# Four score banks at the end of attention, router logits in quarters, and a second sort at the end of the shared stage

## Chip, core and metric

One core of one Trainium2 chip runs the whole program in one launch. The metric is the device time of that core in microseconds.

## What is computed

The input is one sequence of 2048 tokens with 256 features. Two layers run on it; each has an attention part and a feed-forward part, and each part is behind a layer norm that is modulated by a row made from a condition vector, with a gate on its output. In short:

```python
# layer 0; sa, ca, ga, sb, cb, gb come from silu(c0) @ wmod0
h = layernorm(x) * (1 + ca) + sa
x = x + ga * (softmax_attention(h, Wq, Wk, Wv, biases, 16 heads of 16) + h)
h = layernorm(x) * (1 + cb) + sb
probs = softmax(h @ router_w.T)                      # 8 experts, the best 2 of each token, weights renormalised
moe = sum over the 2 experts e of w_e * (silu(h @ gate_e) * (h @ up_e)) @ down_e       # 176 hidden
shared = (silu(h @ s_gate + bg) * (h @ s_up + bu)) @ s_down + bd                       # 352 hidden
x = x + gb * (moe + shared)
# layer 1: relu attention from the first 32 tokens, then a product with a binarised 256 x 256 weight
```

## The kernel before

The tokens are 16 tiles of 128, in 4 chunks of 512 (NC = 4, TPC = 4 tiles a chunk). Attention runs in NU = 16 units: chunk of queries c = u // 4 and group of four heads g = u % 4. A unit has MT = 16 steps t, one for each tile of keys; in this text such a step of the attention is "tile t of unit u". In one, TensorE computes four score products (L683, one for each head, 512 columns, one PSUM bank each), ScalarE takes their exponentials into prob (L1197), and TensorE multiplies the last tile's prob with the values (weigh, L717, or weigh_half, L724, in two halves of 256 columns put between the scores). Beside them TensorE computes score products once more for the maxima (L653) of a unit ahead, and VectorE reduces them (L1419), five tiles ahead (LEAD = 5). The maxima use banks 0 to 3, the scores banks 4, 5 and 6 in turn, and the output gathers in bank 7. In unit 14 the maxima end after tile 10, as there is no unit 16. Unit 15 has none, and its scores go over four banks (4, 5, 6, 3); its first score waits for all exponentials of unit 14. Units 2 to 12 have the product with the values in halves; units 0, 1, 13, 14 and 15 don't.

Each engine works through its queue in the order in which the program is written; semaphores tie the engines together. At the end of attention the next stages begin beside it. The order is written out by hand in hooks (beside_last_but_one, beside_last, beside_shared), and for a chunk c of 512 tokens it is:

- VectorE: statistics(1, c), then POOL: deviation(1, c) (L1970, L1972), then VectorE: normalise(1, c), which writes xh1 (L1359). There is one xh1, so each chunk's comes after the last one's readers.
- TensorE: turn1(c, ft), transposes of xh1 (L778), twice a chunk. VectorE: halves(c, ft) reads them and writes hT_hi and h32 (L1497, L1500). POOL: input_rest(c), the low half hT_lo (L2137).
- TensorE: logits(c), 24 small products of 8 columns each (L800). VectorE: router_logits(c), ScalarE: router_exp(c), VectorE: router_ranks(c) and shares(c).
- POOL: tokens_by_row(c), the rows that are later scattered to the experts' slots.

Beside that, POOL gates and adds the attention of each unit (gate_attention, add_attention, L2060); between the two, SP moves it with 16 small DMAs (move_attention, L402). In the middle of unit 14 POOL also rounds the experts' down weights (down_rounded, L2118 and L2120).

The shared stage has ST * NC = 12 steps n (three parts of the hidden units of each chunk). In each, TensorE computes hidden(sg) and hidden(su) (L837) and the down product of the step before (L858), ScalarE the gate (L1222) and the rounding of the hidden tile (L1227), VectorE the product (L1668) and the low half (L1672). Beside it stand: sort(0) (TensorE at step 1: L871 and L874; VectorE at the same step), chunk 3's statistics, normalise, turns (steps 4 and 5), logits (step 7) and ranks (step 8), and sort(1) (TensorE at step 9, VectorE at step 10). sort(part) counts the chosen tokens of each expert and gives every token its slots: sort(0) for chunks 0 to 2, sort(1) for chunk 3. POOL scatters the rows with indirect DMAs (place, L2180): 24 for part 0, 8 for part 1; after the first six it makes chunk 3's deviation, after 14 chunk 3's input_rest.

Then follow 46 expert tiles (31 of part 0 and 15 of part 1) in a pipeline over all engines: load (xg), transposes (turn_in, L907), gate and up (gate_up, L935), the product (gated_tile, L1686), transposes (turn_hidden, L949), down (down_tile, L961). Beside tiles 8, 10 and 12 TensorE computes the modulation rows of layer 1 (row1, bank 5 or 1) from wmod1. After that come the gather of the results and layer 1.

Bank 4 holds both sorts in turn, then the turned hidden tiles; bank 2 the logits of chunks 0 to 2 and, from step 0 of the shared stage, the up products; bank 5 the turns and logits of chunk 3.

## Time and profile before

| what | us |
|---|---|
| median of 3 runs | 1047.78 (1047.33 to 1050.42) |
| the profiled execution's own time | 1047.59 |
| span in its profile | 1045.8 |
| mean granted TensorE clock | 0.944 of 2.4 GHz |
| units 0 to 15 of attention, first score to the last transpose of output | 105.3 to 772.0 |
| shared stage, up to the first expert tile | to 851.3 |
| expert tiles, up to the last turn of a hidden tile | to 980.3 |

The span is from the first to the last instruction; the execution's own time holds 1.8 us more. In a timeline a row gives start, duration, engine, line, operation, output<-inputs, count, and in brackets the time that the engine sat idle before it and what ended the idling. PE is TensorE, DVE VectorE, ACT ScalarE, POOL GpSimd, SP the engine that only issues DMAs.

### The profile page before, as it was taken

Reading aid. Unit: us, or ns where it says so; the run is one execution under the profiler, and the core shown is the slowest. Engines: PE = TensorE matmul, PEld = TensorE weight load, DVE = VectorE, ACT = ScalarE, POOL = GpSimd, SP = SyncE. Lnnn points to the kernel's source line nnn. Section 1 sums busy time; section 2 is a strip of 40 time slices with the busy share of each in tenths; the row PEclk is TensorE's granted clock in tenths of the full one; section 3 lists DMA queues with packets and bytes.
Section 4 is the critical chain, followed back from the end, with each engine's and each line's share of the span. In section 5 each row is a group of like instructions: output and inputs, shape, how many; then the busy total and the mean of one; then the engine's idle time right before and its main releaser. Section 6 shows DMA issues by size and latency. Waiting matters only on the chain. (4 is left out here: it accounts for less than half of the span.)

```text
span 1045.8 us, 19112 instructions
## 1 busy us (share of the span) xinstructions
PE 988.8 (95%) x6968; PEld 499.5 (48%) x6968; DVE 857.4 (82%) x1162; ACT 675.3 (65%) x1316; POOL 307.4 (29%) x347
## 2 busy tenths in 40 slices
PE   6998999999999999999999999999997889997867
PEld 5453433333333333333333333333456768996656
DVE  5488799999999999999999999987456464655786
ACT  2423777888888888888888888774753224553312
POOL 3285864000000221000000000047437620045553
PEclk8999899999999999999999999996898879997888
DMA  6799200033110110110111101300002224444211
GB/s 197 216 152 134 99 16 6 20 92 106 39 40 6 40 40 7 38 32 16 37 27 21 37 9 39 67 6 1 6 5 70 74 84 144 128 123 135 88 49 60
DMA packets 90129, 65.54 MB, mean 63 GB/s; under 512 B 48406, under 2 KB 77942, under 8 KB 89462
## 3 DMA queue, kind: packets, MB, share of 16 engines
...
q10 hardware_dynamic: 1632, 1.58, 0.5%
...
## 5 line engine op out<-in xcount | busy, mean ns | idle before, releaser
L1197 ACT ACTIVATE prob<-ps 128x512 f32<-128x512 f32 x1024 | 544.6, 599 | 127.7 <-PE ps L683 114.8
L1419 DVE TENSOR_REDUCE mxp<-ps 128x2 f32<-128x1024 f32 x480 | 576.9, 1220 | 22.2 <-PE ps L653 17.4
L683 PE MATMUL ps<-qst,kst 50*128 50x512 f32 x1024 | 374.6, 458 | 5.2 <-DMA qst<-nmT 3.5
L653 PE MATMUL ps<-kst,qst 48*128 48x512 f32 x960 | 328.3, 452 | 0.0
L683 PEld LDWEIGHTS ps<-qst,kst 50*128 50x128 f32 x1024 | 159.7, 190 | 255.2 <-ACT prob L1197 224.6
L724 PE MATMUL ps<-prob,vp 128*32 128x256 f32 x2464 | 196.8, 391 | 0.0
L653 PEld LDWEIGHTS ps<-kst,qst 48*128 48x128 f32 x960 | 130.6, 186 | 14.6 <-issue 6.5
L717 PE MATMUL ps<-prob,vp 128*32 128x512 f32 x816 | 115.6, 640 | 0.0
L724 PEld LDWEIGHTS ps<-prob,vp 128*32 128x32 f32 x2464 | 48.5, 108 | 113.6 <-issue 60.9
L2049 POOL TENSOR_TENSOR att_u<-o_x,rec 128x256 f32<-128x256 f32 x16 | 9.9, 620 | 224.4 <-DVE rec L1444 224.2
L1992 POOL CAST nmp<-nmx 128x16 fp32r<-128x16 f32 x16 | 3.1, 196 | 243.9 <-DVE nmx L1423 218.2
L1686 DVE TENSOR_TENSOR hdt<-ps,sgt 128x176 f32<-128x176 f32 x46 | 15.7, 341 | 49.2 <-ACT sgt L1252 36.4
L1472 DVE TENSOR_REDUCE mxp<-ps 128x2 f32<-128x1024 f32 x32 | 39.2, 1227 | 15.1 <-PE ps L751 15.1
L2210 POOL DMA_INDIRECT yg<-y_slots,slots x32 | 32.1, 1004 | 40.6 <-DVE x L1754 18.5
L1252 ACT ACTIVATE sgt<-ps 128x176 f32<-128x176 f32 x46 | 14.6, 317 | 45.3 <-PE ps L935 36.3
L1359 DVE TENSOR_SCALAR xh<-x,mv,rs 128x256 f32<-128x256 f32 x56 | 34.0, 670 | 9.6 <-POOL rs L1972 9.4
L935 PE MATMUL ps<-gu_hi,th 128*128 x92 | 36.3, 394 | 2.5 <-issue 1.9
L961 PE MATMUL ps<-d_hi,hh 88*128 x92 | 31.3, 340 | 3.7 <-ACT ysb L1265 3.7
L935 PE MATMUL ps<-gu_hi,tl 128*128 x92 | 31.4, 341 | 0.0
L935 PE MATMUL ps<-gu_lo,th 128*128 x92 | 31.3, 340 | 0.0
L1265 ACT ACTIVATE ysb<-ps 128x256 f32<-128x256 f32 x46 | 17.7, 384 | 20.7 <-PE ps L961 16.0
L717 PEld LDWEIGHTS ps<-prob,vp 128*32 128x32 f32 x816 | 16.4, 110 | 28.5 <-ACT prob L1197 18.5
...
## 6 DMA issues: line engine op xcount, KB each, us to landing
...
att_t<-att_u SPq DMA_DIRECT2D x256, 8.0 KB, 1.8
```

The source lines that it names most:

```text
L653: last = nc.tensor.matmul(ps[:, 2 * p + b, :], qst[rows, g, a, P * j:P * (j + 1)], kst[rows, GP * g + a, CH * m:CH * (m + 1)], start=True, ...
L683: nc.tensor.matmul(ps[:, bank, :], kst[rows, GP * g + k // 2, P * t:P * (t + 1)], qst[rows, g, k // 2, :], start=True, stop=True).then_inc ...
L717: last = nc.tensor.matmul(ps[VW * k:VW * (k + 1), 7, :], vp[:, g, t, k, :], prob[:, t % 2, k, :], start=t == 0, stop=t == MT - 1)
L724: last = nc.tensor.matmul(ps[VW * k:VW * (k + 1), 7, cols], vp[:, g, t, k, :], prob[:, t % 2, k, cols], start=False, stop=False, skip_grou ...
L935: last = nc.tensor.matmul(ps[:, 2 + i % 2, 0:2 * I], a[:, i % 2, k, :], b[:].rearrange("p e k n i -> p (e k n i)")[:, bass.ds(e * GW + k * ...
L961: last = nc.tensor.matmul(ps[:, 6, 0:D], a[:, i % 2, n, :], b[:].rearrange("p e n d -> p (e n d)")[:, bass.ds(e * (2 * D) + n * D, D)], st ...
L1197: nc.scalar.activation(prob[:, t % 2, k, :], ps[:, banks[((u * MT if len(banks) == 3 else 0) * G + G * t + k) % len(banks)], :], ACT.Exp, ...
L1265: nc.scalar.activation(ysb[:, i % YB, :], ps[:, 6, 0:D], ACT.Copy).then_inc(yv_s, 1)
L1359: nc.vector.tensor_scalar(dst, x_cols(t), mean, rs, ALU.subtract, ALU.mult).then_inc(xh_s, 1)
L1419: nc.vector.tensor_reduce(own, ps[:, 2 * p:2 * p + 2, :], AX.X, ALU.max).then_inc(mx_read, 1)
L1472: nc.vector.tensor_reduce(own, ps[:, 2 * p:2 * p + 2, :], AX.X, ALU.max).then_inc(mx_read, 1)
L2210: nc.gpsimd.indirect_dma_start(yg[:, m % YG, :], None, y_slots[part], bass.IndirectOffsetOnAxis(ap=slots[:, TPC * d + j, k:k + 1], axis=0) ...
```

## The change

- Attention, units 13 and 14: the products with the values come in halves, for tiles 2 to 15 of unit 13 and 2 to 10 of unit 14.
- Banks: from tile 11 of unit 14 (score 940, RING4) the scores go over four banks (5, 6, 4, 3) without a break into unit 15. The first use of bank 3 waits for the last maximum. The wait for all exponentials at the start of unit 15 is gone.
- Logits of chunks 0 and 1: one tile of 128 tokens (six products) after each of four tiles of unit 15, in place of 24 products after one. The turns of chunk 1 stand one tile earlier. ScalarE's exponentials for the router stand at tiles 7 and 15, in place of 4 and 12.
- VectorE normalises chunk 1 ahead of the logits of chunk 0, and chunk 2 ahead of the logits of chunk 1.
- Logits of chunk 2 go to bank 5, not 2, so that the first up product of the shared stage no longer waits for them to be read; the first turn of chunk 3 into bank 5 does.
- Logits of chunk 3: half before and half after the down product of step 7.
- POOL: chunk 3's deviation after two scatters in place of six.
- Second sort: on TensorE at step 11 in place of 9, in bank 5 at column 128, without the wait for the first sort's slots; on VectorE after the last step, ahead of the first gated tile. The waits for its slots move to the first row1 product.
- SP loads wmod1 without waiting for the second scatters.

```diff
@@ -67,6 +67,7 @@
 QD = 32
 NQ = P // QD
 MAX_LOADS = 2 * NQ
+RING4 = (NU - 2) * G * MT + G * (MI - LEAD)
 
 
 def build(nc, x_in, wq, bq, wk, bk, wv, bv, routerT, gate_w, up_w, down_w, sg_w, sg_b, su_w, su_b,
@@ -325,6 +326,12 @@
         def x_cols(t, n=1):
 
             return x[:].rearrange("p t d -> p (t d)")[:, bass.ds(t * D, n * D)]
+
+        def score_bank(n):
+            return (4, 5, 6)[n % 3] if n < RING4 else (5, 6, 4, 3)[(n - RING4) % 4]
+
+        def sort_cols(part):
+            return (4, 5)[part], 128 * part
 
         END = TPC * (NC - 1)
 
@@ -528,7 +535,6 @@
                     load_tile(i + 6)
                 if i in (0, 2, 4):
                     cols = slice(CH * (i // 2), CH * (i // 2 + 1))
-                    sp.wait_ge(placed[1], 16 * 2 * PARTS[1][1])
                     sp.dma_start(wmod1_sb[:, :, cols], wmod1_v[:, :, cols]).then_inc(mod1_in, 16)
                 if i == 16:
                     sp.wait_ge(row_ps, 3)
@@ -654,7 +660,7 @@
                                             kst[rows, GP * g + a, CH * m:CH * (m + 1)], start=True, stop=True)
                 last.then_inc(mx_ps, 1)
 
-            def unit(u, g, ahead, first=False, beside=None, banks=(4, 5, 6), halved=()):
+            def unit(u, g, ahead, first=False, beside=None, halved=()):
 
                 pe.wait_ge(nm_in, (u + 1) * (16 * MAX_LOADS))
                 for t in range(MT):
@@ -670,17 +676,15 @@
                     pairs = v * (2 * MI) + 2 * i
 
                     def score(k):
-                        n = G * t + k
-                        done = u * (G * MT) + n
-                        bank = banks[(done if len(banks) == 3 else n) % len(banks)]
-                        if len(banks) == 3 and done >= 3:
+                        done = u * (G * MT) + G * t + k
+                        if done == RING4 + 3:
+                            pe.wait_ge(mx_read, NU * (2 * MI))
+                        elif done > RING4 + 3:
+                            pe.wait_ge(p_s, done - 3)
+                        elif done >= 3:
                             pe.wait_ge(p_s, done - 2)
-                        elif n >= len(banks):
-                            pe.wait_ge(p_s, done - len(banks) + 1)
-                        elif n == 0 and not first:
-                            pe.wait_ge(p_s, done)
                         rows = slice(HALF * (k % 2), HALF * (k % 2) + KR + NM)
-                        nc.tensor.matmul(ps[:, bank, :], kst[rows, GP * g + k // 2, P * t:P * (t + 1)],
+                        nc.tensor.matmul(ps[:, score_bank(done), :], kst[rows, GP * g + k // 2, P * t:P * (t + 1)],
                                          qst[rows, g, k // 2, :], start=True, stop=True).then_inc(sc_ps, 1)
 
                     def next_maxima(p):
@@ -769,7 +773,7 @@
             pe.wait_ge(q32_s, len(ITEMS) - EASY)
             unit(0, 0, 2, first=True)
 
-            for u in range(1, NU - 3):
+            for u in range(1, NU - 2):
                 unit(u, u % NG, 2, halved=range(2, MT) if u >= 2 else ())
 
             def turn(q, ft, bank, src):
@@ -786,13 +790,14 @@
             def hT_pair(part, k, c):
                 return (hT_hi[:, c, k, :], hT_lo[:, (c * KT + k) * CH:(c * KT + k + 1) * CH])[part]
 
-            def logits(c, bank, col):
-
-                pe.wait_ge(h_lo_s, KT * (c + 1))
-                pe.wait_ge(tables_s, 2)
-                if c:
-                    pe.wait_ge(lg_s, c)
-                for j in range(TPC):
+            def logits(c, bank, col, tiles=range(TPC)):
+
+                if 0 in tiles:
+                    pe.wait_ge(h_lo_s, KT * (c + 1))
+                    pe.wait_ge(tables_s, 2)
+                    if c:
+                        pe.wait_ge(lg_s, c)
+                for j in tiles:
                     n = 0
                     for k in range(KT):
                         tokens = slice(P * j, P * (j + 1))
@@ -800,9 +805,8 @@
                             last = nc.tensor.matmul(ps[:, bank, col + E * j:col + E * (j + 1)], a[:, tokens], b[:, k, :],
                                                     start=n == 0, stop=n == 3 * KT - 1)
                             n += 1
-                last.then_inc(lg_ps, 1)
-
-            unit(NU - 3, 1, 2)
+                if TPC - 1 in tiles:
+                    last.then_inc(lg_ps, 1)
 
             def beside_last_but_one(t):
                 if t == 15:
@@ -811,18 +815,18 @@
             def beside_last(t):
                 if t == 0:
                     turn1(0, 1)
-                if t == 2:
-                    logits(0, 2, 0)
-                if t in (7, 8):
-                    turn1(1, t - 7)
-                if t == 10:
-                    logits(1, 2, 32)
+                if 2 <= t < 6:
+                    logits(0, 2, 0, (t - 2,))
+                if t in (6, 7):
+                    turn1(1, t - 6)
+                if 10 <= t < 14:
+                    logits(1, 2, 32, (t - 10,))
                 if t in (13, 14):
                     turn1(2, t - 13)
 
-            unit(NU - 2, 2, 1, beside=beside_last_but_one)
-
-            unit(NU - 1, 3, 0, beside=beside_last, banks=(4, 5, 6, 3))
+            unit(NU - 2, 2, 1, beside=beside_last_but_one, halved=range(2, MI - LEAD))
+
+            unit(NU - 1, 3, 0, beside=beside_last)
 
 
             PASSES = ((0, 0), (0, 1), (1, 0))
@@ -865,14 +869,13 @@
 
                 t0, tiles = PARTS[part]
                 pe.wait_ge(chosen_s, (t0 + tiles) // TPC)
-                if part:
-                    pe.wait_ge(slot_s, part)
+                bank, col = sort_cols(part)
                 flat = chosen[:].rearrange("p t e -> p (t e)")
-                nc.tensor.matmul(ps[:, 4, 0:E * tiles], before_bf[:], flat[:, E * t0:E * (t0 + tiles)], start=True, stop=False,
-                                 skip_group_check=True)
+                nc.tensor.matmul(ps[:, bank, col:col + E * tiles], before_bf[:], flat[:, E * t0:E * (t0 + tiles)], start=True,
+                                 stop=False, skip_group_check=True)
                 for t in range(tiles):
-                    last = nc.tensor.matmul(ps[:, 4, E * (t + 1):E * (tiles + 1)].rearrange("p (t e) -> p t e", e=E), ones_bf[:],
-                                            chosen[:, t0 + t, :].unsqueeze(1).to_broadcast([P, tiles - t, E]),
+                    last = nc.tensor.matmul(ps[:, bank, col + E * (t + 1):col + E * (tiles + 1)].rearrange("p (t e) -> p t e", e=E),
+                                            ones_bf[:], chosen[:, t0 + t, :].unsqueeze(1).to_broadcast([P, tiles - t, E]),
                                             start=False, stop=t == tiles - 1, skip_group_check=True)
                 last.then_inc(sort_ps, 1)
 
@@ -883,19 +886,21 @@
             pe.wait_ge(p_s, NU * G * MT)
             weigh(NG - 1, MT - 1)
             hidden((sg_hi, sg_lo), 0, 1).then_inc(g_ps, 1)
-            logits(2, 2, 64)
+            logits(2, 5, 64)
 
             def beside_shared(n):
                 if n == 1:
                     sort(0)
                 if n in (4, 5):
-                    if n == 5:
+                    if n == 4:
+                        pe.wait_ge(lg_s, NC - 1)
+                    else:
                         pe.wait_ge(h_full_s, KT * (NC - 1) + 1)
                     turn(ln(1, NC - 1), n - 4, 5, xh1)
                 if n == 7:
                     pe.wait_ge(h_full_s, KT * NC)
-                    logits(NC - 1, 5, 0)
-                if n == 9:
+                    logits(NC - 1, 5, 0, range(0, TPC // 2))
+                if n == 11:
                     sort(1)
 
             def turn_in(i):
@@ -911,12 +916,12 @@
                 if n >= 2:
                     pe.wait_ge(t_s, n - 1)
                     hidden((sg_hi, sg_lo), 0, n).then_inc(g_ps, 1)
-                if n == 0:
-                    pe.wait_ge(lg_s, NC - 1)
                 hidden((su_hi, su_lo), 2, n).then_inc(u_ps, 1)
                 beside_shared(n)
                 if n >= 1:
                     down(n - 1)
+                if n == 7:
+                    logits(NC - 1, 5, 0, range(TPC // 2, TPC))
 
             pe.wait_ge(t_s, ST * NC - 1)
             turn_in(0)
@@ -944,7 +949,7 @@
                 if i:
                     pe.wait_ge(hl_s, i)
                 else:
-                    pe.wait_ge(slot_s, 2)
+                    pe.wait_ge(slot_s, 1)
                 for n in range(2):
                     last = nc.tensor.transpose(ps[0:IH, 4, P * n:P * (n + 1)], hdt[:, i % 2, IH * n:IH * (n + 1)], ident[:])
                 last.then_inc(ht_ps, 1)
@@ -966,6 +971,7 @@
 
             def row1(j):
                 if j == 0:
+                    pe.wait_ge(slot_s, 2)
                     pe.wait_ge(t_s, ST * NC)
                     pe.wait_ge(mod1_in, 48)
                     pe.wait_ge(cb_ready, 2)
@@ -1186,7 +1192,7 @@
                 act.wait_ge(lg_s, c + 1)
                 nc.scalar.activation(pr[:], lg[:], ACT.Exp).then_inc(exp_s, 1)
 
-            def unit(u, first, ahead, exps={}, banks=(4, 5, 6)):
+            def unit(u, first, exps={}):
                 for t in range(MT):
                     if t in exps:
                         router_exp(exps[t])
@@ -1194,14 +1200,12 @@
                         act.wait_ge(sc_ps, u * (G * MT) + G * t + k + 1)
                         if k == 0 and not (first and t < 2):
                             act.wait_ge(pv_s, u * MT + t - 1)
-                        nc.scalar.activation(prob[:, t % 2, k, :], ps[:, banks[((u * MT if len(banks) == 3 else 0) * G + G * t + k) % len(banks)], :], ACT.Exp,
+                        nc.scalar.activation(prob[:, t % 2, k, :], ps[:, score_bank(u * (G * MT) + G * t + k), :], ACT.Exp,
                                              scale=DH ** -0.5).then_inc(p_s, 1)
 
-            unit(0, True, 2)
-            for u in range(1, NU - 2):
-                unit(u, False, 2)
-            unit(NU - 2, False, 1)
-            unit(NU - 1, False, 0, exps={4: 0, 12: 1}, banks=(4, 5, 6, 3))
+            for u in range(NU - 1):
+                unit(u, u == 0)
+            unit(NU - 1, False, exps={7: 0, 15: 1})
 
             def gate_up_rounded(i):
 
@@ -1553,8 +1557,9 @@
                 t0, tiles = PARTS[part]
                 s, first_tile = sorts[part], TILES[0] * part
                 own_rank = rank[:, t0:t0 + tiles, :]
-                earlier_tokens = ps[:, 4, 0:E * tiles].rearrange("p (t e) -> p t e", e=E)
-                tokens_of = ps[:, 4, E * tiles:E * (tiles + 1)]
+                bank, col = sort_cols(part)
+                earlier_tokens = ps[:, bank, col:col + E * tiles].rearrange("p (t e) -> p t e", e=E)
+                tokens_of = ps[:, bank, col + E * tiles:col + E * (tiles + 1)]
                 first = s["first"]
                 dve.wait_ge(sort_ps, part + 1)
                 rt_then(nc.vector.scalar_tensor_tensor(s["over"][:], tokens_of.unsqueeze(2).to_broadcast([P, E, tiles]), 1.0 / P,
@@ -1600,18 +1605,20 @@
             statistics(1, 1)
             dve.wait_ge(zero_in, 16 * ZERO_DMAS)
             dve.wait_ge(tables_s, 3)
-            router(0, 2, 0)
+            normalise(1, 1)
+            router_logits(0, 2, 0)
+            both_halves(1)
+            router_ranks(0)
             shares(0)
-            normalise(1, 1)
-            both_halves(1)
             statistics(1, 2)
-            router(1, 2, 32)
+            normalise(1, 2)
+            router_logits(1, 2, 32)
+            both_halves(2)
+            router_ranks(1)
             shares(1)
-            normalise(1, 2)
-            both_halves(2)
             leave_output(NU - 1)
             invert_sums(NU - 1)
-            router(2, 2, 64)
+            router(2, 5, 64)
 
             def gate_up_rest(i):
 
@@ -1654,9 +1661,6 @@
                     router_ranks(NC - 1)
                 if n == 9:
                     gate_up_rest(3)
-                if n == 10:
-                    sort(1)
-
             for n in range(ST * NC):
                 s = n % ST
                 rows = S_ROWS[s]
@@ -1870,6 +1874,7 @@
             shares(NC - 1)
             add_shared(NC - 1)
             input_rest(1)
+            sort(1)
             for i in range(TS + 2):
                 if i < TS:
                     gated_tile(i)
@@ -2181,9 +2186,9 @@
                             x_slots[part], bass.IndirectOffsetOnAxis(ap=slots[:, PARTS[part][0] + t, k:k + 1], axis=0),
                             h_tm[part][:, t, :], None).then_inc(placed[part], 16)
 
-            place(0, range(0, 3))
+            place(0, range(0, 1))
             deviation(1, NC - 1)
-            place(0, range(3, 7))
+            place(0, range(1, 7))
             pool.wait_ge(sc_ps, G * MT * NU)
             input_rest(NC - 1)
             place(0, range(7, PARTS[0][1]))
```

## Rows read from the trace of the kernel before

**Rows 1.** The page, part 1: busy us, share of the span, instructions

```profile
PE 988.8 (95%) x6968; PEld 499.5 (48%) x6968; DVE 857.4 (82%) x1162; ACT 675.3 (65%) x1316; POOL 307.4 (29%) x347
```

**Rows 2.** Windows: length, busy us (instructions) by engine, PEclk, DMA share, GB/s

```profile
704.40:724.80 20.40, 19.03 (x67) 5.41 (x67) 16.11 (x7) 9.57 (x19) 15.67 (x6) 0.50 0.01 1
...
796.60:803.30 6.70, 3.77 (x17) 3.76 (x18) 4.53 (x8) 1.30 (x2) 5.41 (x6) 0.50 0.23 80
...
834.10:840.80 6.70, 6.70 (x27) 5.83 (x28) 3.95 (x4) 1.32 (x2) 0.00 (x0) 0.50 0.00 0
```

**Rows 3.** VectorE's timeline, units 11 to 13 end: start us, us

```profile
593.16 0.71 DVE L1440 STREAM_TRANSPOSE o_x<-ps 128x512 f32<-128x512 f32 x1
...
633.11 0.71 DVE L1440 STREAM_TRANSPOSE o_x<-ps 128x512 f32<-128x512 f32 x1
...
674.84 0.71 DVE L1440 STREAM_TRANSPOSE o_x<-ps 128x512 f32<-128x512 f32 x1
```

**Rows 4.** ScalarE's timeline, 703 to 757 us; idle before in brackets

```profile
703.61 2.06 ACT L1197 ACTIVATE prob<-ps 128x512 f32<-128x512 f32 x4 [0.55 <-PE ps L683]
...
707.61 2.08 ACT L1197 ACTIVATE prob<-ps 128x512 f32<-128x512 f32 x4 [1.94 <-PE ps L683]
...
735.36 8.11 ACT L1197 ACTIVATE prob<-ps 128x512 f32<-128x512 f32 x16 [0.75 <-PE ps L683]
...
755.56 2.06 ACT L1197 ACTIVATE prob<-ps 128x512 f32<-128x512 f32 x4 [5.16 <-PE ps L683]
```

**Rows 5.** Timelines of POOL, VectorE and TensorE around chunk 0, 705 to 721 us

```profile
710.25 8.87 POOL L2120 TENSOR_TENSOR d_lo<-d_raw,d_hi 88x4096 fp32r<-88x4096 f32 x1
...
705.73 13.86 DVE L1359 TENSOR_SCALAR xh<-x,mv,rs 128x256 f32<-128x256 f32 x4 [1.58 <-POOL rs L1972]
...
719.64 1.12 PE L778 MATMUL ps<-ident,xh 128*128 128x128 f32 x4 [0.59 <-DVE xh L1359]
```

**Rows 6.** Timelines of POOL and TensorE, second logits and chunk 2

```profile
747.38 0.74 POOL L2060 TENSOR_TENSOR x<-x,att_t 128x256 f32<-128x256 f32 x1 [12.06 <-DMA att_t<-att_u]
...
750.75 0.27 PE L800 MATMUL ps<-rw_hi,hT_hi 128*128 128x8 f32 x1 [0.76 <-POOL hT_lo L2137]
...
763.91 0.63 PE L778 MATMUL ps<-ident,xh 128*128 128x128 f32 x4 [1.73 <-DVE xh L1359]
```

**Rows 7.** Timelines of TensorE, VectorE and POOL in the shared stage

```profile
776.10 0.79 PE L837 MATMUL ps<-hT_hi,su_hi 128*128 128x512 f32 x1 [0.74 <-DVE lg L1516]
...
791.70 0.38 DVE L1344 BATCH_NORM_AGGREGATE mv<-bn_st 128x2 f32<-128x6 f32 x4
...
796.91 1.05 POOL L1972 TENSOR_TENSOR rs<-veps,m 128x4 f32<-128x4 f32 x1
...
799.53 1.12 PE L778 MATMUL ps<-ident,xh 128*128 128x128 f32 x4 [5.35 <-DVE xh L1359]
...
811.86 1.30 POOL L2137 TENSOR_TENSOR hT_lo<-h32b,hT_hi 128x512 fp32r<-128x512 f32 x1
...
814.83 0.17 PE L800 MATMUL ps<-rw_hi,hT_hi 128*128 128x8 f32 x1
```

**Rows 8.** Timelines of ScalarE and TensorE, steps 8 and 9

```profile
827.66 0.69 ACT L1222 ACTIVATE sig<-ps,bg 96x512 f32<-96x512 f32 x1 [7.37 <-remote]
...
834.07 0.21 PE L871 MATMUL ps<-chosen,before_bf 128*128 128x32 bf16 x1 [4.84 <-DVE chosen L1534]
```

**Rows 9.** Timelines of VectorE and TensorE, second sort and first tiles

```profile
844.58 0.18 DVE L1560 SCALAR_TENSOR_TENSOR over<-ps,count 128x32 f32<-128x32 f32 x1
...
847.33 0.16 DVE L1577 TENSOR_SCALAR owner<-ends 1x15 int32<-1x15 f32 x1
...
848.92 0.74 PE L858 MATMUL ps<-sd_hi,hid_hi 96*128 96x256 f32 x4 [1.36 <-ACT hid_hi L1227]
...
853.81 0.34 DVE L1686 TENSOR_TENSOR hdt<-ps,sgt 128x176 f32<-128x176 f32 x1 [0.73 <-issue]
...
856.06 0.63 PE L949 MATMUL ps<-ident,hdt 128*88 128x128 f32 x2
```


## The prediction

> **What bounds the kernel now.** I read the page first. TensorE is busy 95% of the span, VectorE 82%, ScalarE 65% [rows 1]. That is an average over stages, and the change touches only the stretch from about 633 to 860 us, so the other views were read for that stretch alone.
>
> The stage windows show the granted clock. From 704.4 to 724.8 us, the tail of unit 14 and the head of unit 15 of the attention, it is 0.50, which is 1.2 GHz. So it is in windows of 6.7 us in the shared stage [rows 2]. In each of them TensorE waits or has just waited.
>
> The starts of the transposes of attention output give the length of a unit. Unit 12, with the product in halves, takes 633.11 - 593.16 = 39.95 us. Unit 13, without halves, takes 674.84 - 633.11 = 41.73 us [rows 3]. So 14 halved tiles save 1.78 us, 0.127 us a tile.
>
> ScalarE's timeline shows the three banks. In unit 14's tail, at the low clock, a tile takes 1.94 us of idle and 2.08 of exponentials, 4.0 us. In unit 15, on four banks already, 16 exponentials run without a gap in 8.11 us, 2.03 us a tile. Around the second logits ScalarE is idle for 5.16 us [rows 4].
>
> The rows that decide most are those on what TensorE waits for when a normalised chunk is turned. xh of chunk 0 takes VectorE 13.86 us for four small operations, and it ends, at 719.59, just after POOL's rest of the down weights, which alone takes 8.87 us. TensorE turns the chunk at 719.64 after only 0.59 us of waiting [rows 5]. The other waits stand below with their steps.
>
> **The change, part by part.** The profiled execution took 1047.59 us by its own time, 1.8 over its span of 1045.8. The median of the runs shown is 0.2 above it. The sum is made against 1047.6, and 0.2 is added at the end.
>
> *Halves in units 13 and 14.* 14 tiles of unit 13 and 9 of unit 14 at 0.127 us [rows 3] make 1.78 + 1.14 = 2.9 us. VectorE's last maximum comes that much earlier, and with it the deviation, xh and POOL's rounding, which all hang on it. Bounds: 2.5 to 3.2. I take 2.9.
>
> *Four banks from tile 11 of unit 14.* ScalarE's tile 12 ends at 703.61 + 2.06 = 705.67 [rows 4]. Halves and two tiles of 2.03 in place of 2.61 bring that to 701.6; three more tiles and the product behind them, and TensorE would reach the turn of chunk 0 near 708.5. But the turn needs xh, and xh ends with POOL's rounding, at 719.6 - 2.9 = 716.7 [rows 5]. TensorE stands idle for some 8.2 us, and the four banks give nothing there. What is late next is everything behind the turn: the rest of chunk 0, the first logits, the tokens by row, the gate of unit 14. Value 0; bounds 0 and 8.2 gained.
> The Trainium skill, page "SBUF — State Buffer", section "Who interferes with whom", says that a VectorE operation in a two-port mode and a POOL operation lock a shared port pair for a whole instruction, and that the later one is blocked. By that rule the order on the two engines would have to change to free xh, and it doesn't; the trace agrees, since xh ends where POOL does. Were there no lock, the sum would be 8.2 us lower.
>
> *The last unit, up to the second logits.* These wait for POOL's rest of chunk 1, which stands behind the addition of unit 14's attention at 747.38, for which POOL idles 12.06 us while SP moves it in 16 DMAs [rows 6]. That chain is counted from the turn of chunk 0 and holds no work of TensorE's that the change shortens. So the first quarter starts at 750.75 - 2.9, as now. The first logits in quarters and the earlier xh of chunk 1 fill time that is then waited for: TensorE is there some 3 us early. Value 0, bounds -1 and +1.
>
> *From the second logits to the turn of chunk 2.* Now 763.91 - 750.75 = 13.16 us, the last 1.73 of it idle for xh [rows 6], since VectorE normalises chunk 2 only after ranks and shares. With the change xh comes first, and between lie four quarters and three tiles. ScalarE's idle 5.16 us [rows 4] less TensorE's own 0.76 makes 1.1 us a quarter, partly at 1.2 GHz; I estimate 0.7 at the full clock. Three tiles at 2.03 and four quarters make 8.9 us; with a window of 6.7 us at half rate in it, 12.2. I take 10.2, which is 3.0 gained, bounds 1 and 4.3.
>
> *Logits of chunk 2 in bank 5.* The wait of 0.74 us ahead of the first up product goes [rows 7]. Sort and first down product behind it need the ranks and the rounded hidden tile, which hang on the same logits; 0.3 at most gets through. Counted as 0.
>
> *Deviation of chunk 3 after one tile's scatters instead of three.* TensorE waits 5.35 us for xh at 799.53. VectorE's statistics end at 792.08 and POOL's deviation only at 797.96, behind six scatters [rows 7]. With four scatters fewer, xh comes some 3.6 us earlier, allowing VectorE its work between. But the last logits, at 814.83, need POOL's rest of chunk 3, which ends at 813.16 [rows 7] behind 14 scatters in all, in either order. POOL even idles 0.9 us for the statistics. So TensorE meets the wait again ahead of the logits, some 4 us of it. Kept: the 1.67 us of slack less 0.9, 0.7 us; bounds 0 and 3.
>
> *Second sort on TensorE at step 11, not 9.* TensorE waits 4.84 us for the ranks, because ScalarE's gate of step 8 came after 7.37 us of a wait that the trace puts down as remote [rows 8]. Without the sort there, the down product of step 8 needs the rounded hidden tile, some 0.7 us after TensorE gets there if ScalarE is as late again: 4.1 gained. The low-clock window behind the wait, 6.7 us [rows 2], costs 3.4; I count half, 1.7, since another can arise behind the new wait ahead of the logits. Together 5.8, bounds 1 and 8.2.
>
> *Second sort on VectorE at the stage's end.* The idle 1.36 us ahead of the last down product goes, as its hidden tile waited for the sort: 1.4 gained. In its new place the sort, 844.58 to 847.49, so 2.9 us, stands ahead of the first gated tile. That one is ready at 854.15 and is wanted at 856.06 [rows 9], so its turn is 1.0 us late, and the tiles behind it as much. 1.0 lost, bounds 0 and 2.9. POOL's second scatters move with the sort by some 9 us; the first tile that reads them is number 31 of 46. SP no longer waits for them ahead of wmod1, which is wanted at tile 8: hidden either way, and at worst nothing, since the wait only goes. The wait for the second slots now stands ahead of the first row product, at tile 8, past the sort by six tiles: hidden.
>
> Sum: 2.9 + 0 + 0 + 3.0 + 0 + 0.7 + 5.8 + 1.4 - 1.0 = 12.8 us. 1047.6 - 12.8 + 0.2 = 1035.0 us. The tile stage and the end behind it move as a whole.
>
> **The rivals.**
> *The tail opens* (0.10). xh isn't the bound, or TensorE no longer idles and the clock stays up. For it: tiles of 2.03 us in unit 15 [rows 4]. Against it: rows 5. It gives up to 8.2 us more: 1026.8 us. The page "TensorE: Matmul & The Clock Gate" of the Trainium skill, section "Terms", puts the penalty at the throttled time times the share taken away; for the windows of rows 2, 33.8 us, that is an estimate of 17 us, if all went. The trace doesn't bear this out, as in the tail half of each tile was a wait between engines.
>
> *The waits only move in the shared stage* (0.20). POOL's 12 scatters in a row, and last logits split by a down product, make the last ranks as late as before, and the stall of step 9 turns up at step 8 or 11. The 5.8 goes: 1040.8 us.
>
> *Only the halves count* (0.08). Each later gain ends at a wait for POOL, and 2.9 us or little more is left: 1045 us.
>
> *The clock stays low* (0.04), the slower side. TensorE's idle 8.2 us ahead of the turn leaves it at 1.2 GHz, and unit 15 never brings it back. A tile at that clock takes 4.0 us with its waits, 2.0 over ScalarE's 2.03; four banks take away about half of that. 1.0 us over 16 tiles, and 24 router matmuls twice at twice their price, lose some 20 us: 1055 us. It turns the sign from 13 tiles at the low clock. Against it: the clock was back 5.2 us after the turn at 719.64, and 3.8 us after the wait of 5.35 [rows 2, 5, 7].
>
> **How the numbers follow.** The forecast has 0.58. The range leaves out half of the opened tail (0.05) below, and above it "only the halves", the low clock and a little of the moved waits (0.15): 1028 to 1042. Within 0.3% (3.1 us, about what a measurement here can tell from no change) means above 1044.6, half of "only the halves" and a little of the moved waits. That makes faster 0.90, same 0.06, slower 0.04.
>
> **What would show it.** In the changed profile: transposes of attention output 1.8 us closer for unit 13; ScalarE's tiles at 2.03 in unit 14's tail; then TensorE idle 7 to 9 us for xh, its turn near 716.7; the second logits near 748; the turn of chunk 3 after 1 to 2 us of waiting, and a new wait for POOL's rest ahead of the last logits; no wait at the second sort; a gap ahead of the first turn of a hidden tile. I am wrong if xh isn't waited for, if the last logits don't wait, or if more than two low-clock windows come or go.

## The result and the profile after

The changed kernel takes 1052.57 us (median of 18 runs, 1049.37 to 1057.86), the kernel before 1047.49 in its 18 runs of the same comparison. The ratio is 1.0057, with a 95% interval of 1.0041 to 1.0073: slower by 0.57%, some 6 us, where 12.8 us less was forecast. The profiled execution took 1053.04 us, with a span of 1051.3.

The page, part 1, of the changed kernel. TensorE is busy for 979.4 us, 9.4 less than before [rows 1], in a longer span: it makes the same products (more of them in halves) and waits more.

```profile
PE 979.4 (93%) x7152; PEld 495.2 (47%) x7152; DVE 869.1 (83%) x1162; ACT 678.6 (65%) x1316; POOL 307.8 (29%) x347
```

What was forecast for the halves is there. Timelines of TensorE, VectorE and POOL around chunk 0, which answer to [rows 5]:

```profile
714.60 1.11 PE L782 MATMUL ps<-ident,xh 128*128 128x128 f32 x4 [8.89 <-DVE xh L1363]
...
700.74 13.80 DVE L1363 TENSOR_SCALAR xh<-x,mv,rs 128x256 f32<-128x256 f32 x4 [1.58 <-POOL rs L1977]
...
705.26 8.81 POOL L2125 TENSOR_TENSOR d_lo<-d_raw,d_hi 88x4096 fp32r<-88x4096 f32 x1
```

Counted from the transpose of unit 12's output, TensorE turns chunk 0 after 83.78 us, before after 86.53. It waits 8.89 us for xh (8.2 forecast). The clock is at 1.2 GHz then, but back at 2.4 GHz some 6 us after the turn.

At the second logits, those of chunk 1, it goes wrong for the first time. TensorE's timeline, and ScalarE's, which answers to [rows 4]:

```profile
746.08 0.37 PE L805 MATMUL ps<-rw_hi,hT_hi 128*128 128x8 f32 x1 [3.23 <-POOL hT_lo L2142]
...
751.83 1.22 PE L687 MATMUL ps<-qst,kst 50*128 50x512 f32 x4
752.98 1.93 PE L721 MATMUL ps<-prob,vp 128*32 128x512 f32 x8
754.85 0.38 PE L805 MATMUL ps<-rw_hi,hT_hi 128*128 128x8 f32 x1
...
756.22 1.22 PE L687 MATMUL ps<-qst,kst 50*128 50x512 f32 x4
...
760.54 1.11 PE L782 MATMUL ps<-ident,xh 128*128 128x128 f32 x4
```

```profile
748.28 2.07 ACT L1203 ACTIVATE prob<-ps 128x512 f32<-128x512 f32 x4 [4.86 <-PE ps L687]
752.66 2.06 ACT L1203 ACTIVATE prob<-ps 128x512 f32<-128x512 f32 x4 [2.32 <-PE ps L687]
757.05 2.06 ACT L1203 ACTIVATE prob<-ps 128x512 f32<-128x512 f32 x4 [2.32 <-PE ps L687]
```

The windows of the changed kernel (length, busy us and instructions by engine, PEclk, DMA share, GB/s). They answer to [rows 2].

```profile
744.40:764.90 20.50, 18.82 (x78) 9.18 (x79) 3.81 (x13) 8.37 (x17) 8.79 (x7) 0.50 0.00 1
706.80:720.50 13.70, 5.90 (x24) 2.63 (x24) 10.68 (x6) 2.06 (x4) 8.54 (x2) 0.50 0.00 0
```

In the first of them the clock is at 1.2 GHz for 20.5 us, though TensorE never idles again from 746.08 to its end. A tile there takes 756.22 - 751.83 = 4.39 us, its products with the values 1.93. The clock comes back only behind the last quarter. In the kernel before, the same stretch has one low window of some 6.8 us; it begins at 752.1, in the middle of the whole logits. The quarters of chunk 0, at the full clock, were cheap: a tile with one took 726.49 - 724.07 = 2.42 us (starts of two quarters on TensorE), 0.4 more than the 2.03 of a tile without.

Ranks and shares of chunk 1 on VectorE, and what POOL does meanwhile (it makes tokens by row of chunk 2):

```profile
768.38 2.55 DVE L1533 TENSOR_TENSOR cmp1A<-pr 128x256 f32<-128x256 f32 x1
770.85 2.57 DVE L1534 TENSOR_TENSOR cmp2A<-pr 128x256 f32<-128x256 f32 x1
773.46 0.42 DVE L1535 TENSOR_TENSOR cmp2A<-cmp2A,tri 128x256 f32<-128x256 f32 x1
...
776.62 0.72 DVE L1444 STREAM_TRANSPOSE o_x<-ps 128x512 f32<-128x512 f32 x1
```

```profile
768.25 2.40 POOL L2133 TENSOR_TENSOR h_tmA<-xh,rows 128x1024 f32<-128x1024 f32 x1
770.73 2.42 POOL L2135 TENSOR_TENSOR h_tmA<-h_tmA,rows 128x1024 f32<-128x1024 f32 x1
```

Two comparisons of one shape take 2.55 and 2.57 us as long as POOL's two operations last, and the next operation 0.42. The whole piece, from 766.84 to 776.59, takes 9.75 us; in the kernel before it took 4.6. The output of unit 15 and the last router stand behind it. TensorE's timeline shows what that does to the shared stage; the second and third row answer to [rows 7].

```profile
781.74 0.22 PE L874 MATMUL ps<-chosen,before_bf 128*128 128x96 bf16 x1 [3.67 <-DVE chosen L1538]
...
799.46 0.63 PE L782 MATMUL ps<-ident,xh 128*128 128x128 f32 x4 [0.88 <-DVE xh L1363]
...
817.45 0.35 PE L805 MATMUL ps<-rw_hi,hT_hi 128*128 128x8 f32 x1 [4.25 <-issue]
```

The wait of 5.35 us at the turn of chunk 3 is down to 0.88, and 4.25 us of it are met again ahead of the last logits (POOL's rest ends at 817.35), as forecast. The wait of 4.84 us at the second sort [rows 8] is gone.

Last, the first expert tiles: POOL's second scatters (the first and the last of eight), ScalarE and VectorE. They answer to [rows 9].

```profile
854.02 1.01 POOL L2185 DMA_INDIRECT x_slots<-h_tmB,slots  x1 [18.64 <-DVE slots L1577]
...
862.92 0.96 POOL L2185 DMA_INDIRECT x_slots<-h_tmB,slots  x1 [0.30 <-issue]
```

```profile
859.06 0.33 PE L940 MATMUL ps<-gu_hi,tl 128*128 x1
...
864.08 0.32 ACT L1256 ACTIVATE sgt<-ps 128x176 f32<-128x176 f32 x1 [3.92 <-PE ps L940]
865.49 0.38 ACT L1262 ACTIVATE hh<-ps 88x256 fp32r<-88x256 f32 x1 [1.09 <-remote]
```

```profile
864.43 0.34 DVE L1690 TENSOR_TENSOR hdt<-ps,sgt 128x176 f32<-128x176 f32 x1 [5.75 <-ACT sgt L1256]
```

TensorE's product of the tile ends at 859.39 by its record, and ScalarE, which only waits for it, starts at 864.08, 4.7 us later. These are the 5 us of the stage: from the third to the eleventh tile 26.1 us for 20.9. Counted from unit 12, the gate of the first expert tile comes at 220.2 us where before had 220.4. So in this pair of profiles all gains and losses ahead of the tiles cancel, and the whole difference of some 5 us lies in the first eleven tiles.

### The profile page after: what moved, and what is told of

Read it like the earlier page. It is cut to its first block and busy times, and to the rows that moved or that the text cites. A ratio compares the mean times of both kernels' runs of the same rounds, so it can differ in the third digit from the quotient of the medians.

```text
span 1051.3 us, 19480 instructions
## 1 busy us (share of the span) xinstructions
PE 979.4 (93%) x7152; PEld 495.2 (47%) x7152; DVE 869.1 (83%) x1162; ACT 678.6 (65%) x1316; POOL 307.8 (29%) x347
## 5 line engine op out<-in xcount | busy, mean ns | idle before, releaser
L687 PE MATMUL ps<-qst,kst 50*128 50x512 f32 x1024 | 370.2, 454 | 1.3 <-DMA qst<-nmT 1.3
L659 PE MATMUL ps<-kst,qst 48*128 48x512 f32 x960 | 333.2, 450 | 0.0
L687 PEld LDWEIGHTS ps<-qst,kst 50*128 50x128 f32 x1024 | 156.4, 188 | 231.6 <-ACT prob L1203 207.7
L728 PE MATMUL ps<-prob,vp 128*32 128x256 f32 x2832 | 226.2, 391 | 0.0
L728 PEld LDWEIGHTS ps<-prob,vp 128*32 128x32 f32 x2832 | 55.7, 108 | 130.6 <-issue 70.1
L721 PE MATMUL ps<-prob,vp 128*32 128x512 f32 x632 | 90.2, 645 | 0.0
L2215 POOL DMA_INDIRECT yg<-y_slots,slots x32 | 32.4, 1012 | 39.3 <-DVE x L1758 17.1
L2185 POOL DMA_INDIRECT x_slots<-h_tmA,slots x24 | 25.8, 1075 | 7.2 <-issue 6.6
## 6 DMA issues: line engine op xcount, KB each, us to landing
kst<-k_parts SPq DMA_DIRECT2D x18, 256.0 KB, 11.6
```

Of the source, the lines that this page charges most:

```text
L659: last = nc.tensor.matmul(ps[:, 2 * p + b, :], qst[rows, g, a, P * j:P * (j + 1)], kst[rows, GP * g + a, CH * m:CH * (m + 1)], start=True, ...
L687: nc.tensor.matmul(ps[:, score_bank(done), :], kst[rows, GP * g + k // 2, P * t:P * (t + 1)], qst[rows, g, k // 2, :], start=True, stop=Tr ...
L721: last = nc.tensor.matmul(ps[VW * k:VW * (k + 1), 7, :], vp[:, g, t, k, :], prob[:, t % 2, k, :], start=t == 0, stop=t == MT - 1)
L728: last = nc.tensor.matmul(ps[VW * k:VW * (k + 1), 7, cols], vp[:, g, t, k, :], prob[:, t % 2, k, cols], start=False, stop=False, skip_grou ...
L2185: nc.gpsimd.indirect_dma_start(x_slots[part], bass.IndirectOffsetOnAxis(ap=slots[:, PARTS[part][0] + t, k:k + 1], axis=0), h_tm[part][:, t ...
L2215: nc.gpsimd.indirect_dma_start(yg[:, m % YG, :], None, y_slots[part], bass.IndirectOffsetOnAxis(ap=slots[:, TPC * d + j, k:k + 1], axis=0) ...
```

## The experiments

Sixteen kernels in one frame. The profiled executions, us between events: second logits to the turn of chunk 2, that to the first hidden product, that to the slots of the first sort, the product on VectorE of step 8 to the first expert tile's gate, and the gates of expert tiles 0 to 2, 2 to 10 and 10 to 30. The ratios are to the kernel before on the same chip.

```
                          logits turn   hidden step 8 tiles  tiles  tiles  ratio (95%)
                          -turn  -hidd. -slots -tile0 0-2    2-10   10-30
before                    13.16   4.62  18.61  25.09  5.85   20.92  48.49
changed                   14.46   6.54  22.39  21.87  6.27   26.06  48.15  1.0057 (1.0041-1.0073)
halves alone              11.65   4.62  18.63  25.33  6.53   21.49  48.58  0.9979 (0.9960-0.9997)
changed, sort back        14.44   7.21  22.06  29.40  5.12   20.65  48.69  1.0047 (1.0026-1.0068)
changed, output first     14.46   6.43  22.78  21.95  6.24   26.12  48.77  1.0042 (1.0022-1.0061)
whole logits              11.31   4.66  22.36  20.20  6.23   26.15  48.66  0.9997 (0.9973-1.0022)
 + ranks back             11.66   4.63  18.60  18.91  7.16   24.95  48.56  0.9979 (0.9957-1.0001)
 + ranks and sort back    11.72   5.98  18.62  26.59  5.11   20.57  48.26  0.9972 (0.9953-0.9991)
 + ranks back, held       11.66   4.63  18.61  18.11  6.22   19.73  56.06  0.9990 (0.9966-1.0015)
second logits whole       13.67   4.97  22.36  20.22  6.22   26.13  48.69  1.0010 (0.9992-1.0028)
first logits whole        13.04   7.09  22.17  20.20  6.23   25.88  48.50  1.0024 (1.0006-1.0041)
 + ranks back, spread     12.83   4.62  18.62  20.19  6.20   19.94  48.49  0.9898 (0.9868-0.9927)
 + ranks back, none       11.65   4.63  18.62  18.89  6.34   19.61  48.67  0.9912 (0.9890-0.9934)
before, spread            12.17   4.88  18.60  24.55  4.35   20.06  48.46  0.9982 (0.9955-1.0010)
changed, spread           14.08   6.15  22.38  19.47  7.15   19.95  48.14  1.0027 (1.0000-1.0053)
 + spread, rest earlier   11.66   5.96  18.62  26.23  6.23   19.99  48.58  0.9913 (0.9886-0.9941)
```

"+" stands for the kernel with whole logits. 0.001 is 1.05 us. Each row of columns is one profiled execution: the kernels with ranks back, held, spread and none are the same up to the turn of chunk 2, and their first column is still 11.65 to 12.83, by the length of the low stretch (3.4 or 6.8 us) that the execution had.

**Halves alone.** The kernel before with one part of the change.

```diff
-            unit(NU - 3, 1, 2)
+            unit(NU - 3, 1, 2, halved=range(2, MT))
...
-            unit(NU - 2, 2, 1, beside=beside_last_but_one)
+            unit(NU - 2, 2, 1, beside=beside_last_but_one, halved=range(2, MI - LEAD))
```

> The kernel before with the products in halves in units 13 and 14 alone. My forecast's first term: the unit's transposes 1.8 us closer for unit 13, VectorE's last maximum, xh of chunk 0 and its turn 2.9 us earlier, and all of it kept to the end: ratio 0.997, about 1044.6 us where before has 1047.5. If instead the stages behind absorb it (waits for POOL in the shared stage, another pattern of low-clock windows), the turn of chunk 0 is 2.9 us earlier and the end is within 1 us of before.

1045.11 us, 0.9979. The turn of chunk 0 comes at 83.80, as in the changed kernel. This term was right: 2.2 us for 2.9 (the interval leaves 0.3 to 4.2).

**The sort back.** The changed kernel with sort(1) at step 9 on TensorE and step 10 on VectorE.

> The changed kernel with the second sort back at step 9 on TensorE and step 10 on VectorE; all else as changed. Theory C (the late sort puts POOL's second scatters beside the first expert tiles, where TensorE's signals come 4 to 6 us late): the scatters go back ahead of or into the first two tiles and the time falls by 3 to 6 us against the changed kernel. Rival (what is lost, is lost before the shared stage): no change, or 1 to 3 us slower, since the wait for the ranks is back.

1051.9 us, 1.0047: 1 us, inside the intervals, where 3 to 6 were expected. The gap in the tiles went, as expected (20.65 us for 26.06), though SP's early load of wmod1 stayed. The columns tell why so little is gained: the late sort wins 29.40 - 21.87 = 7.5 us up to the first tile and loses 26.06 - 20.65 + 6.27 - 5.12 = 6.6 in the ten behind.

**The output first.** The changed kernel, with leave_output and invert_sums of unit 15 ahead of ranks and shares of chunk 1 on VectorE.

> The changed kernel with VectorE taking the output of unit 15 ahead of the ranks and shares of chunk 1. Theory A (ranks and shares, 9.75 us beside POOL's rows, hold the output up by some 5 us, and with it the gate, the 16 moves, the addition and all of the first scatters): the addition of unit 15's attention comes 3 to 5 us earlier against the hidden stage's start, and the time falls by 2 to 5 us. Rival (the router's own chain, logits to ranks of chunk 2, is what the first down product waits for): the addition comes earlier, but the first sort is as late or later, and the time changes by less than 1 us.

1051.36 us, 1.0042. The addition of unit 15's attention came 5.7 us earlier, but the ranks of chunk 2, and so sort and first down product, did not, as the rival said: VectorE now waits 2.85 us for the output first, and though ranks and shares of chunk 1 then take 7.3 us for 9.75, it is no earlier at the router of chunk 2.

**Whole logits.**

```diff
-                if 2 <= t < 6:
-                    logits(0, 2, 0, (t - 2,))
+                if t == 2:
+                    logits(0, 2, 0)
...
-                if 10 <= t < 14:
-                    logits(1, 2, 32, (t - 10,))
+                if t == 10:
+                    logits(1, 2, 32)
```

> The changed kernel with the logits of chunks 0 and 1 whole again, after tiles 2 and 10 of unit 15; all else as changed. Theory B (quarters among four tiles hold TensorE at the low clock for 20.5 us where whole logits hold it there for 6.8): the low window behind the second logits is 7 to 10 us, the turn of chunk 2 comes 3 to 5 us earlier after the logits' start, and the time falls by 2 to 5 us. Rival (the low window comes from the idle wait for POOL's rest of chunk 1, which whole logits have too): the window stays at 14 to 20 us, and the time is within 1 us of the changed kernel's.

1047.5 us, 0.9997. The same products, only not spread over four tiles, take back all that the change had lost, as theory B said, and this step of 6.3 us stands clear of the intervals. TensorE's wait ahead of the second logits is 1.26 us instead of 3.23, and the low window behind it is 6.8 us instead of 20.5:

```profile
751.80:758.60 6.80, 6.80 (x33) 3.82 (x36) 4.60 (x17) 2.58 (x6) 4.36 (x4) 0.50 0.00 0
```

**One chunk whole, the other in quarters.** Two kernels complete the square: the second logits whole, and the first logits whole.

> The whole change (1052.6 us), with the logits of chunk 1 alone whole again after tile 10; those of chunk 0 stay in quarters. Theory B: only the quarters of chunk 1 cost, since they lie in the stretch at half clock (744.4 to 764.9 us, 4.38 us a tile), while those of chunk 0 ran at full clock at 2.4 us a tile: the time is that of the kernel with both whole, 1047.5 us within 0.7, and the low clock behind the wait ahead of the second logits lasts 3.4 to 6.8 us instead of 20.5. Rival: quarters cost at either place, some 2.5 us each set: 1050 us.

> The whole change (1052.6 us), with the logits of chunk 0 alone whole again after tile 2; those of chunk 1 stay in quarters. It is the fourth corner beside both in quarters (1052.6), first in quarters and second whole (1048.7) and both whole (1047.5). Theory B2: the quarters of chunk 0 bring TensorE to the second logits early, it idles 3.2 to 3.8 us there instead of 1.3, and the clock falls behind it at 744 to 746 us; the quarters of chunk 1 then keep it low for 20.5 us, where whole logits end it after 13.7 or 6.8. Without the early idle the low stretch is 13.7 us or less and the time 1050 us, 1 to 1.5 above both whole, turn of chunk 2 some 12.5 to 13.5 us after the second logits begin. Rival: the quarters of chunk 1 cost what they cost wherever the clock starts to fall, the low stretch is 20.5 us again, 1051.5 us.

1048.69 us (1.0010) and 1052.38 us (1.0024; the kernel before was at 1049.07 beside it, so this is 1050.0 us on the scale of the expectations). With the corners: none in quarters -0.3 us to the kernel before, the first alone +1.0, the second alone +2.5, both +6.0. Beside quarters of the other chunk each set costs: the first 3.5 us, the second 4.9, both give or take 2.5. Alone, against none in quarters, they cost 1.4 and 2.8 give or take 3, which isn't secured. The low windows, of the second logits whole and of the first logits whole:

```profile
746.40:760.10 13.70, 13.70 (x59) 6.74 (x59) 1.86 (x7) 6.20 (x12) 5.18 (x4) 0.50 0.00 0
```

```profile
752.30:769.40 17.10, 17.10 (x74) 8.04 (x66) 6.41 (x19) 7.80 (x17) 5.27 (x5) 0.50 0.01 1
```

PE is busy for the whole of either window. Where the first logits were in quarters, TensorE idled 3.57 us ahead of the second, and the window is 13.7 us even with whole logits; where they were whole, it idled 1.79 and the quarters behind still made 17.1. The first kernel's time lies between those of theory and rival. The forecast of a stretch of 3.4 to 6.8 us for it fell, and so did that of 13.7 us or less for the second. What the quarters of chunk 1 do shows in all sixteen profiles: the low stretch at the second logits is 17.1 or 20.5 us in the five kernels that have them, and 3.4 to 13.7 in the eleven that have these logits whole. The part of the early idle is less sure. It rests on the one profile with 13.7 us, and the changed kernel with its scatters spread, the same up to here, had 17.1 us where the changed one had 20.5, so one execution's length says little.

**Ranks back, both back.** The kernel with whole logits, with the order of before on VectorE (and ScalarE's router exponentials ahead of tiles 4 and 12, and the turns of chunk 1 again at tiles 7 and 8), without and with the sort back. The edit on VectorE:

```diff
-            normalise(1, 1)
-            router_logits(0, 2, 0)
-            both_halves(1)
-            router_ranks(0)
+            router(0, 2, 0)
             shares(0)
+            normalise(1, 1)
+            both_halves(1)
             statistics(1, 2)
+            router(1, 2, 32)
+            shares(1)
             normalise(1, 2)
-            router_logits(1, 2, 32)
             both_halves(2)
-            router_ranks(1)
-            shares(1)
```

> The kernel with whole logits (1047.5 us), with ranks and shares of chunks 0 and 1 back ahead of the normalising of the next chunk on VectorE, and ScalarE's two router exponentials back ahead of tiles 4 and 12. Theory A: in the changed order ranks and shares of chunk 1 run beside POOL's tokens by row, 9.75 us for some 5.0, and hold the output of unit 15 and the last router back. Measured from unit 12, the ranks of chunk 2 come at 145.67 us with whole logits and at 142.48 with the halves alone, so this kernel should gain 3.2: 1044.3 us, ranks of chunk 2 near 142.5, ranks and shares of chunk 1 in some 5 us, the addition of unit 15's attention 4 to 6 us earlier. Rival: POOL's rest of chunk 3, ahead of the last logits, is the bound anyway and takes the gain back: 1047 us, last logits still near 180.9.

> The kernel with whole logits and the ranks back, and the second sort back at step 9 on TensorE and step 10 on VectorE too. What is left of the change is halves, four banks, logits of chunk 2 in another bank, the early deviation and the last logits in two parts. Theory C: the late second sort wins 3.3 us up to the first expert tile and loses 4.2 in tiles 2 to 5, where POOL's second scatters now lie and TensorE's signals come late: this kernel is within 1 us of the one with the ranks back alone, 1043.5 to 1044.5 us, with tiles 2 to 5 in 8 us and no gap of more than 2 us there. Rival: without the quarters the late sort pays as forecast, some 4 us: this kernel is then 3 to 4 us slower than the one with the ranks back alone, 1048 us.

1044.67 us (0.9979) and 1044.77 us (0.9972). The first hidden product to the slots takes 18.60 us for 22.36; the run time gave 1.9 of these 3.8 us, and the intervals of the two ratios overlap. The last logits came 4.6 us earlier, counted from unit 12, so POOL's rest of chunk 3 didn't take the gain back. Ranks and shares of chunk 1 take 4.6 us (752.73 to 757.32); their comparisons, with POOL idle:

```profile
753.39 0.43 DVE L1533 TENSOR_TENSOR cmp1A<-pr 128x256 f32<-128x256 f32 x1
753.74 0.42 DVE L1534 TENSOR_TENSOR cmp2A<-pr 128x256 f32<-128x256 f32 x1
```

The Trainium skill, page "SBUF — State Buffer", section "Who interferes with whom", says that a VectorE instruction with two inputs in SBUF contends with a POOL instruction that reads SBUF. The rows agree: 2.55 us beside POOL, 0.43 without.

The late sort is worth nothing that the runs can tell without the quarters either, as theory C said: 26.59 - 18.91 = 7.7 us won up to the first tile, and 6.4 lost in tiles 0 to 10.

**Scatters held, spread, left out.** All three start from the kernel with whole logits and the ranks back, late sort kept. POOL's eight second scatters are held in a row until tile 12, spread in pairs, or left out with the waits for them.

```diff
 # held
+            pool.wait_ge(tin_ps, 12)
             place(1, range(PARTS[1][1]))
 # spread
-            place(1, range(PARTS[1][1]))
+            for t in range(PARTS[1][1]):
+                pool.wait_ge(tin_ps, 3 * (t + 1))
+                place(1, (t,))
```

> The kernel with whole logits and the ranks back (late sort kept), with POOL's second scatters held until TensorE has turned the twelfth expert tile. They are needed by the load of tile 31. Theory D: TensorE's signals come 3 to 6 us late while POOL's scatters are under way, so with the scatters the gap of tiles 2 to 5 (13.2 us for 8.1) moves to tiles 12 to 15, and the time stays that of the kernel with the ranks back within 1 us, or gains up to 2 if the pipeline hides more of it there. Rival: the gap has nothing to do with the scatters (the sort ahead of the first gated tile, or the low clock, makes it): it stays at tiles 2 to 5 and nothing shows at tiles 12 to 15.

> The kernel with whole logits and the ranks back (1044.7 us, late sort kept), with POOL's eight second scatters spread: a pair each behind the turn of expert tiles 3, 6, 9 and 12. Theory D: TensorE's signals are held until the scatters under way have landed, 5 to 6 us for eight in a row; a pair lands within some 3.5 us and holds a signal for at most 2, part of which the tile pipeline hides, so that 2 to 4 us are won: 1041 to 1043 us. Rival: each pair holds as much as its share of the row, and the sum is the same: 1044.7 us. Second rival: every pair costs a whole hold of 4 us: 1050 us or more.

> The kernel with whole logits and the ranks back (1044.7 us), with the eight second scatters and the waits for them left out: tiles 31 to 45 multiply zeros, and no time but that of the scatters goes. It prices what the second scatters cost there. Theory D: the gap of expert tiles 2 to 5 (12.3 us for 8.1) goes, and the stage is 4 us shorter: 1040.5 us, with no late signal of TensorE behind the first tile. Rival: the gap is of the stage's start (buffers, the late sort ahead of the first gated tile, the low clock), and stays: 1044.5 us.

Held: 1045.7 us, 0.9990. The gap is gone from tiles 2 to 10 (19.73 us) and stands in tiles 10 to 30 (56.06), and the time is within its interval of the kernel with the ranks back, as theory D said; its rival is out. ScalarE's and POOL's timelines of this kernel:

```profile
869.48 0.38 ACT L1269 ACTIVATE ysb<-ps 128x256 f32<-128x256 f32 x1 [2.00 <-remote]
875.26 0.32 ACT L1256 ACTIVATE sgt<-ps 128x176 f32<-128x176 f32 x1 [5.40 <-remote]
```

```profile
865.16 1.01 POOL L2183 DMA_INDIRECT x_slots<-h_tmB,slots  x1 [39.71 <-PE ps L912]
...
874.08 0.96 POOL L2183 DMA_INDIRECT x_slots<-h_tmB,slots  x1 [0.30 <-issue]
```

Spread: 1037.73 us (6 runs), 0.9898, faster than the 1041 to 1043 expected. Left out: 1040.15 us, 0.9912. Tiles 2 to 10 take 19.94 and 19.61 us: in pairs the scatters cost nothing that can be seen there, in a row 5 to 7.5 us in every profile where the row begins behind the first tile's gate. Timelines of POOL and ScalarE with the scatters spread:

```profile
851.10 0.96 POOL L2183 DMA_INDIRECT x_slots<-h_tmB,slots  x1 [3.52 <-PE ps L912]
852.36 0.96 POOL L2183 DMA_INDIRECT x_slots<-h_tmB,slots  x1 [0.30 <-issue]
857.97 0.96 POOL L2183 DMA_INDIRECT x_slots<-h_tmB,slots  x1 [4.65 <-PE ps L912]
```

```profile
850.42 0.32 ACT L1256 ACTIVATE sgt<-ps 128x176 f32<-128x176 f32 x1 [0.82 <-PE ps L940]
...
852.66 0.32 ACT L1256 ACTIVATE sgt<-ps 128x176 f32<-128x176 f32 x1 [0.72 <-PE ps L940]
...
855.17 0.32 ACT L1256 ACTIVATE sgt<-ps 128x176 f32<-128x176 f32 x1 [0.78 <-PE ps L940]
```

A gate every 2.2 to 2.5 us, through the pair at 851.10. The gain by run time, 8.5 us from 0.9979 to 0.9898, is more than the 5.0 of the profile (and the two ratios come from different comparisons), so its size is only known to be 3 us or more: the intervals leave 3.0 to 14.

**The same edit in the two kernels, and POOL's rest earlier.** The spread scatters put into the kernel before (without SP's wait for them ahead of wmod1, which else locks the two) and into the changed kernel; and POOL's rest of chunk 3 behind 10 of the first scatters, not 14, in the kernel with whole logits, ranks back and spread scatters.

> The kernel before with its second scatters spread, a pair each behind the turn of expert tiles 3, 6, 9 and 12, and without SP's wait for them ahead of wmod1; nothing else. The hold of TensorE's signals falls there on the change from shared to expert stage (855.6 to 858.6 us), where a stall is there anyway. Theory D with the place: in the kernel before the row of scatters costs 1 to 3 us, so this gives a ratio of 0.997 to 0.999 to it. Rival: the row costs some 6 us wherever it lies, so that the late sort had no part in the loss: ratio 0.994.

> The whole change with its second scatters spread, a pair each behind expert tiles 3, 6, 9 and 12; quarters and the order of ranks are left as changed. Theory: the row of scatters costs 5 us in the changed kernel, in expert tiles 2 to 5, so the ratio to the kernel before falls from 1.0057 to some 1.001, and tiles 2 to 5 take 7 to 8 us for 13.2. Rival: the low clock after the sort takes some of it back: 1.003.

```diff
-            place(0, range(1, 7))
+            place(0, range(1, 5))
             pool.wait_ge(sc_ps, G * MT * NU)
             input_rest(NC - 1)
-            place(0, range(7, PARTS[0][1]))
+            place(0, range(5, PARTS[0][1]))
```

> The kernel with whole logits, ranks back and spread scatters (ratio 0.990), with POOL's rest of chunk 3 behind 10 of the first scatters instead of 14. The second half of the chunk stands ready at 799.7 us, and POOL takes it up at 807.15 after more scatters, so that TensorE waits 4.3 us ahead of the last logits. If POOL's order is what the last logits wait for, they start up to 4.3 us earlier and the ratio falls to 0.986 to 0.989. Rival: the scatters that now lie behind, or the ranks behind the last logits, take it back: 0.990.

The kernel before with spread scatters is at 1044.2 us, 0.9982, the changed one at 1048.02 us, 1.0027. In tiles 0 to 10 spreading wins 26.77 - 24.41 = 2.4 us before and 32.33 - 27.10 = 5.2 in the changed kernel. So in these profiles the row of scatters cost something before too, and the late sort doubled it. The run times give 1.9 us before, as forecast, but the interval reaches no change; and they give 3.1 us in the changed kernel (1.0057 to 1.0027), less than the 5 forecast, with intervals that overlap. Why it is less isn't known.

With the rest earlier the kernel takes 1035.07 us, 0.9913. TensorE's timeline: the wait ahead of the last logits is gone and another has come.

```profile
804.08 0.17 PE L805 MATMUL ps<-rw_hi,hT_hi 128*128 128x8 f32 x1
...
825.60 1.22 PE L862 MATMUL ps<-sd_hi,hid_hi 128*128 128x256 f32 x4 [3.07 <-DVE x L1633]
```

ScalarE's timeline of it, the gate of a step of the shared stage:

```profile
822.85 0.69 ACT L1226 ACTIVATE sig<-ps,bg 128x512 f32<-128x512 f32 x1 [10.14 <-remote]
```

The last logits begin 3.5 us earlier and the ranks behind them come 11.6 us earlier, counted from unit 12, but the first expert tile only 2.2: in steps 8 to 10 signals are late until the first scatters have landed, at 822.4; the gate above waits 10.14 us. By its run time it can't be told from the kernel without this edit, as the rival said. Both beat the kernel before by some 0.9 to 1.0%, and the changed kernel by 1.4 to 1.6%.

## Why the prediction was wrong

The terms, as forecast and as the ratios of a chain of kernels give them. The chain adds up by its making, and a step between two ratios is known to 2 to 3.5 us. So the quarters' row is clear of the noise, the halves' just so (their ratio is taken straight to the kernel before), and the others aren't:

| part | forecast, us | measured, us | from |
|---|---|---|---|
| halves | -2.9 | -2.2 | halves alone |
| four banks, bank 5, early deviation, last logits in parts | -0.7 | -0.7 | both back against halves alone |
| second sort late | -6.2 | +0.7 | ranks back against both back |
| xh of the next chunk ahead of the ranks, and what moves with it | in the next row | +1.9 | whole logits against ranks back |
| quarters | -3.0 for both rows | +6.3 | changed against whole logits |
| sum | -12.8 | +6.0 | |

**Right.** The halves; the four banks swallowed by the wait for xh (8.89 us for 8.2) behind POOL; the wait of chunk 3 that is met again ahead of the last logits (4.25 us for 4); no wait at the second sort. Of the rivals, "the tail opens" is out. "The waits only move in the shared stage" was right in that the late sort brought nothing, but not in its reason: the wait did go, and the loss came in the tiles. "The clock stays low" named the sign and a part of the mechanism but not the place: 8.89 us of idle ahead of the turn of chunk 0 left no lasting low clock, while the stretch behind the 3.23 us ahead of the second logits stayed low for 20.5.

**From the second logits to the turn of chunk 2** is the first step that failed: "I estimate 0.7 at the full clock. Three tiles at 2.03 and four quarters make 8.9 us; with a window of 6.7 us at half rate in it, 12.2. I take 10.2". It took 14.46, more than before. The price of a quarter was not the fault (0.4 us at the full clock, in chunk 0, for the 0.7 estimated). The length of the low window was: it was taken from the kernel before, where the logits are whole. With the same 24 products in pieces between tiles that TensorE bounds at 1.2 GHz, the clock stayed down for 20.5 us. The first logits in quarters were counted as "value 0" too. They cost 3.5 us beside the second, give or take 2.5; they bring TensorE early to a wait, 3.23 us for 1.26, and a longer wait was priced at nothing. That this wait lengthens the low stretch is likely but rests on one profile.

With whole logits and the new order the stretch takes 11.31 us, and 12.83 to 13.16 in the kernels with the order of before and a low window as long, 6.8 us. So xh ahead of the ranks did gain some 1.5 to 1.8 us here, of the forecast's kind. How much of the 6.3 us is the clock's and how much the pieces' own is not separated: no kernel here had quarters of chunk 1 at the full clock.

**"0.3 at most gets through"** to sort and first down product is the second. It looked at where the logits of chunk 2 lie and not at VectorE's queue ahead of them: ranks and shares of chunk 1 were moved to just where POOL makes tokens by row, and the router of chunk 2 stands behind them. It took 9.75 us instead of 4.6, and TensorE waited 3.67 us at the first sort. With the order of before, the stretch from the first hidden product to the slots is 3.8 us shorter, of which the run times show 1.9, inside their noise.

**The late second sort** is the third. The wait at step 9 went, as forecast, and 7.7 us were won up to the first tile. But "POOL's second scatters move with the sort by some 9 us; the first tile that reads them is number 31 of 46" priced only the wait for the data. Eight scatters in a row came with late signals of TensorE in each of the places where they were put. Before, most of that fell on the change of stages; the forecast's own row of a "remote" wait of 7.37 us [rows 8], which ends at 827.66, 0.9 us after the first scatters have landed, was the sign of it, and it was taken for a delay of ScalarE.
